# Reordering GpSimd's weight split, the stacking DMAs and the low parts of x in a decoder layer's attention

## The reference, cut to what matters

```
x = x + attention(layernorm(x), W_qkv, W_out)
  q, k, v = split(xn @ W_qkv)            # 16 heads of 64
  q, k = rotary(q), rotary(k)            # pairs of columns: x1*cos - x2*sin, x1*sin + x2*cos
  w = softmax(mask(q @ k.T / 8))         # causal
  out = (w @ v) @ W_out
x = x + memory_attention(layernorm(x), ctx)   # a scan over 64 context rows builds the memory
x = x + experts(layernorm(x))
```

## Time and profile before

| | |
|---|---|
| median of three runs | 2825.81 us |
| the profiled execution | 2824.66 us |
| its span | 2822.9 us |
| mean granted TensorE clock | 0.975 |
| TensorE busy | 2640.8 us (94%) |
| VectorE busy | 2004.1 us (71%) |
| ScalarE busy | 1620.0 us (57%) |
| GpSimd busy | 1497.6 us (53%) |

### The profile page before, as it was taken

One profiled execution on the slowest core, in us unless ns is written; L12 is line 12 of the kernel. 1 busy time (PEld: TensorE's weight loads), 2 busy tenths in 40 slices (PEclk: granted clock), 3 DMA queues, 4 the chain that ended last, 5 costly groups with the idle time before them and its releaser, 6 DMA issues. The chain is left out here.

```text
span 2822.9 us, 51923 instructions
## 1 busy us (share of the span) xinstructions
PE 2640.8 (94%) x16935; PEld 2336.0 (83%) x16935; DVE 2004.1 (71%) x4219; ACT 1620.0 (57%) x3158; POOL 1497.6 (53%) x1680
## 2 busy tenths in 40 slices
PE   8999989999899999899997799999969999999997
PEld 5888878888788888788886677778759999999997
DVE  6777777777767777777776688879856666666665
ACT  3666666666756666666665533333326666666665
POOL 3676746666556766577653334434424444444444
PEclk9999999999999999999998899999979999999999
DMA  6544443535443545343535454545334434444433
GB/s 170 115 116 116 108 121 91 123 99 128 115 100 88 132 103 125 101 113 84 117 75 139 119 180 144 146 131 149 116 132 104 102 74 89 102 103 104 104 53 52
DMA packets 192360, 316.56 MB, mean 112 GB/s; under 512 B 60496, under 2 KB 106224, under 8 KB 189104
## 3 DMA queue, kind: packets, MB, share of 16 engines
q1 hardware_dynamic: 148656, 216.86, 31.1%
q0 software_dynamic: 43520, 97.46, 14.0%
HBM read 241.08 MB, written 75.17 MB: 112 GB/s over the span
## 5 line engine op out<-in xcount | busy, mean ns | idle before, releaser
L1171 ACT ACTIVATE a_pt<-a_PT 128x512 fp32r<-128x512 f32 (+3 forms) x768 | 350.3, 490 | 466.1 <-PE a_PT L1030 461.0
L1316 DVE TENSOR_TENSOR a_pt<-a_PT,a_pt 128x512 fp32r<-128x512 f32 (+3 forms) x768 | 401.0, 549 | 154.2 <-ACT a_pt L1171 150.4
L1306 DVE CUSTOM_DVE_ANT_0 a_S<-a_S,a_mask 128x1024 f32<-128x1024 f32 (+7 forms) x512 | 386.9, 756 | 80.1 <-PE a_S L1019 78.7
L1160 ACT ACTIVATE a_pb<-a_S,a_nmax 128x1024 f32<-128x1024 f32 (+7 forms) x512 | 379.9, 742 | 26.4 <-DVE a_nmax L1306 24.5
L1030 PE MATMUL a_PT<-early_ident,a_pb 128*128 128x128 f32 x2304 | 342.9, 276 | 55.6 <-DVE a_pt L1316 55.2
L1030 PEld LDWEIGHTS a_PT<-early_ident,a_pb 128*128 128x128 f32 x2304 | 274.5, 142 | 111.5 <-issue 68.6
L1047 PE MATMUL a_O<-a_pt,a_v 128*128 128x256 f32 (+1 forms) x2560 | 344.6, 282 | 8.1 <-DVE a_xt L1291 5.3
L1047 PEld LDWEIGHTS a_O<-a_pt,a_v 128*128 128x128 f32 x2560 | 328.5, 192 | 20.8 <-DVE a_xt L1291 11.1
L1018 PE MATMUL a_S<-a_kh,a_qs 128*128 128x512 f32 (+3 forms) x768 | 283.0, 369 | 21.7 <-DMA a_kl<-early_rot 21.0
L2215 POOL DMA_INDIRECT early_stage<-in_we,e_ix x119 | 128.6, 1081 | 276.9 <-issue 140.1
L1019 PE MATMUL a_S<-a_kl,a_qs 128*128 128x512 f32 (+3 forms) x768 | 259.0, 349 | 0.0
(11 more groups left out here) (332 smaller groups left out, 7610.0 us busy)
## 6 DMA issues: line engine op xcount, KB each, us to landing
a_qs<-early_rot SPq DMA_DIRECT2D x256, 128.0 KB
a_kh<-early_rot SPq DMA_DIRECT2D x256, 128.0 KB
a_kl<-early_rot SPq DMA_DIRECT2D x256, 128.0 KB
m_hn<-scr_hs SPq DMA_DIRECT2D x40, 516.0 KB
scr_attT<-a_ot SPq DMA_DIRECT2D x256, 64.0 KB, 2.2
early_stage<-in_wqk POOLq DMA_DIRECT2D x31, 512.0 KB, 4.1
m_att<-scr_attT SPq DMA_DIRECT2D x30, 512.0 KB
m_rb<-scr_rinv SPq DMA_DIRECT2D x60, 256.0 KB
```

Source lines behind the costliest of these rows:

```text
L1160: act.activation(pb[u % 2][:, 0:cols], S[u % 2][:, 0:cols], ACT.Exp, bias=nmax[:, u % GU:u % GU + 1], scale=-1.0, accum_out=rsum[:, b % 2, ...
L1171: act.activation(pt[u % 2][:, 0, 4 * s:4 * s + m, (qt % 2) * P:(qt % 2 + 1) * P], PT[(k + s) % 2][:, 0:m * P].rearrange("p (k q) -> p k q" ...
L1306: dve.tensor_tensor_reduce(out=sc, in0=sc, in1=mask[:, T - cols:T], scale=-1.0, scalar=-MASKED, op0=ALU.add, op1=ALU.min, accum_out=nmax[: ...
L1316: dve.tensor_tensor(pt[u % 2][:, 1, 4 * s:4 * s + m, q], PT[(k + s) % 2][:, 0:m * P].rearrange("p (k q) -> p k q", k=m), pt[u % 2][:, 0, 4 ...
```

## The change

Five edits, all in the attention phase. On SP, a stack's first six DMAs wait for the rotation's high parts and the last six for the low parts. On GpSimd, the load behind the very first weight split waits for the first stack, and `load_next` for the stack of head 62; weights are split at the head of a step, ahead of the rotation's additions and low parts, while the loads behind x's parts keep their place. On ScalarE, before the loop, the values' first two high copies stand between and behind the two rotation copies and ahead of the weight copy. On VectorE, x's low parts move behind the values' and the probabilities' low parts of the step.

```diff
             def stack(hg):
                 i, sl = hg // 2, hg % 2
-                sp.wait_ge(s_rot, 4 * (i + 1))
                 if hg >= 2:
                     sp.wait_ge(s_sfull, QT * (hg - 1))
                 for r in range(4):
+                    if r == 0:
+                        sp.wait_ge(s_rhi, 4 * (i + 1))
+                    if r == 2:
+                        sp.wait_ge(s_rot, 4 * (i + 1))
                     sp.dma_start(qs[r * 32:r * 32 + 32, sl, :].bitcast(F32),
...
                 if p in ridx and ridx[p] + 2 < len(by_raw):
+                    if p == pieces[0]:
+                        gp.wait_ge(s_stack[0], 192)
                     load(ridx[p] + 2)
...
                 gp.wait_ge(s_wlow, len(wcount))
+                gp.wait_ge(s_stack[0], 192 * (last + 1))
                 for k in range(6):
...
             for u in range(U + 2):
+                for p in splits(u):
+                    if p[0] != "x":
+                        low(p)
                 for i, j in ends(q_steps(u - 1), 4):
                     if j % 2:
                         rope_add(i, j // 2)
...
                 for p in splits(u):
-                    low(p)
+                    if p[0] == "x":
+                        low(p)
...
             rope_high(0, 0)
+            v_high(0, 0)
             rope_high(0, 1)
+            v_high(0, 1)
             high(pieces[0])
-            for j in range(4):
+            for j in range(2, 4):
                 v_high(0, j)
...
                     tile_stats(tile_in(u, 4))
-                if 0 < u < U:
-                    for p in splits(u - 1):
-                        if p[0] == "x":
-                            x_low(p)
                 for i, j in ends(q_steps(u - 1), 4):
                     if j < 3:
                         rope_mult(i, j)
...
                 if 2 <= u < U + 2:
                     part_low(u - 2)
+                if 0 < u < U:
+                    for p in splits(u - 1):
+                        if p[0] == "x":
+                            x_low(p)
```

## The result

The changed kernel takes 2853.93 us (median of six runs, 2849.48 to 2855.60) against 2827.80 for the kernel before on the same chip (six runs, 2821.13 to 2831.80): ratio 1.0092, 95% interval 1.0077 to 1.0107. It is slower by 26 us; 2850 was forecast. The profiled execution of after has a span of 2852.3 us and a granted clock of 0.976, that of before 2822.9 and 0.975.

The account below looks back on a forecast made before the run. TensorE, busy 94% of the span, was taken to bound the kernel. Terms +46.1, +4, -10.7, -1.4, -10.0, -1.5 and -2 gave +24.5 us, 2850 on the median; 2822 to 2868 for eight times in ten.

Parts of the forecast that it names:

- The swap: Weight split ahead of GpSimd's additions: ScalarE's rotation copy comes late, delaying TensorE's product with the probabilities; +46.1 us.
- Rival 1: ScalarE's delay doesn't reach TensorE, the 0.12 us slack being a misreading; only the gains are left, 2800 us; chance 0.14.
- rival 2: Half the swap's delay arrives, TensorE making up the rest in its small waits; 2823 to 2838 us; chance 0.18.
- The 23 pairs: Ordinary pairs of heads in attention where the swap's delay reaches TensorE: 1.99 to 2.28 us each, together 48.4 us.
- The clock: TensorE's new idle gaps of 2 us can take its clock down; +4 us, at most 32.
- Rival 3: The clock falls in most of TensorE's new gaps; 2870 us or more; chance 0.06.
- Stacks: Stacking DMAs start on high parts, so eight head-change waits go: -10.7 us, and -1.4 for the clock's dip at 501.
- The end: Six loads wait for head 62's stack, so TensorE's wait near 1540 nearly goes; -10.0 us.
- The room of 2 us: At the end, the six loads run beside the last stack with about 2 us to spare; otherwise up to 9.8 return.
- rival 4: The three-megabyte load collides with the last stack: 9.8 us come back, 2859 us; chance 0.07.
- The opening: TensorE's 2.04 us wait at 57.48 goes with the values' copy earlier, projections end sooner; -1.5 us (0 to -2.5).
- The turns: Three batch turns: TensorE's waits shrink with x's low parts behind the probabilities', 0.7 us per turn; -2 us (0 to -9).

Follow-up runs that it names:

- load_behind: The changed kernel with the weight split still first, but the load that follows it issued behind the rotation's additions; 2823.91 us, ratio 0.9992 to the kernel before.
- no_swap: The changed kernel with GpSimd's old order put back (rotation's additions first, then weight split and load); 2801.93 us, ratio 0.9909 to the kernel before.
- swap_only: The kernel before with only the weight split moved ahead of the rotation's additions on GpSimd; 2868.08 us, ratio 1.0141.
- stack_only: The kernel before with only the stacks' split wait (first six DMAs on the high parts, last six on the low parts); 2808.84 us, ratio 0.9929.
- end_only: The kernel before with only the six 512 KB loads for the following phase waiting for head 62's stack; 2823.58 us, ratio 0.9977.
- x_only: The kernel before with only x's low parts moved behind the probabilities' low parts on VectorE; 2824.45 us, ratio 0.9988.
- swap_at_turns: The changed kernel with the weight split ahead of the additions only at the three batch turns, GpSimd's old order elsewhere; 2802.19 us, ratio 0.9902.

## Why the prediction was right

**The swap** was priced at 46.1 us plus 4 for the clock, 50.1; it measured 52. The step-by-step sum held in its parts: split to additions 3.26 us (3.35 forecast), wait of the copy 1.86 (2.05), gap of TensorE 1.80 to 2.0 (1.95), 0.10 us between VectorE's end and TensorE's start (0.12). The gap is that of 21 pairs. Rival 1, that this small slack was an artefact of modelled ends, falls with the gaps; rival 2, that half is made up in TensorE's small waits, falls with load_behind: even a delay of 0.94 us arrives whole. The 23 pairs were the right ones, and the six at and behind the turns swallowed their delay. One step was misread: all 23 pairs were priced with a load behind the split, and the last two (heads 58 and 60) have none, so 0.92 and 1.25 us arrived there in place of 1.9 and 2.2. The other 21 heads were priced at 42.0 us and grew by 43.3 without the dips. Their gaps are 39.5 of these; where TensorE lost the other 0.2 us a head isn't shown.

**The clock.** Of the 52.0 us the five heads with a dip hold 1.3 us each over their neighbours, 6.5 in all, against 4 forecast; the price of a dip (1.4) was right, and 45.5 remain for the gaps, against 46.1. Rival 3, a dip in most gaps, falls: behind 18 of the 23 gaps there was none.

**Stacks.** -12.1 forecast with the dip at 501. The eight heads between 6 and 42 gained 13.7 us in no_swap (18, the one with the dip, 3.45), so the term was right there. What the prediction didn't see is that the swap takes the same waits away: swap_only costs 40 us with the old stacks, which is 52 less these 12. So the two terms hold only as a pair. The swap's 50 is its price beside the stack edit, and beside the swap the stack edit is worth nothing at these heads. Alone in before the edit is worth 20 [14, 26]; a part of what it gained beyond the term, 3.0 us, lies at the end: 1.23 at head 62, where a stack that starts earlier meets the six loads earlier (8.5 us of waiting instead of 9.8), and 1.75 at head 63, the low clock's tail of before that stack_only hasn't. The SP queue ran as worked out: rotation copy 295.86, first stack DMA 3.2 us later (3.1 forecast), the last six 7.0 us later (7.0):

```profile
299.07 0.57 SPq L709 DMA_DIRECT2D a_qs<-early_rot  x1
...
302.86 0.59 SPq L709 DMA_DIRECT2D a_qs<-early_rot  x1
303.49 1.24 SPq L713 DMA_DIRECT2D a_kl<-early_rot  x2
```

**The end.** -10.0 forecast; -6.5 by the times of end_only, with 10 inside its interval, and 8.3, 9.9 and 8.6 us in heads 62 and 63 together of after, no_swap and end_only. The size was near, but two errors met. The room of 2 us for loads and last stack together wasn't enough, and a wait of 2.73 us stands in after, over a fourth of rival 4. Against it, the low clock behind the wait of before cost 1.75 us more than the 0.9 that was put in the sum. Before TensorE's first scores of the last head in after:

```profile
1566.97 3.18 POOL L897 DMA_DIRECT2D early_stage<-in_wmem  x6 [11.21 <-DMA a_kl<-early_rot]
...
1586.61 0.50 PE L1028 MATMUL a_S<-a_kh,a_qs 128*128 128x512 f32 x1 [2.73 <-DMA a_kl<-early_rot]
```

**The opening.** -1.5 forecast; heads 0 to 2 of after took 2.0 more (no_swap's 1.2), and alone it is nothing (+3 us at ratio 1.0011, zero within the interval). Taken from no_swap's heads, this is the term that was mis-sized most, by 2.7 us. Answers to the earlier trace rows:

```profile
55.18 1.23 DVE L1255 TENSOR_TENSOR scan_keys<-scan_keys,a_rT 128x1024 f32<-128x1024 f32 x1
...
64.02 0.50 PE L972 MATMUL a_Z<-early_xT,early_wq 128*128 128x512 f32 x1 [1.86 <-DVE a_v L1308]
...
95.57 0.33 PE L1040 MATMUL a_PT<-early_ident,a_pb 128*128 128x128 f32 x1 [3.70 <-DVE a_pt L1328]
```

The 2.04 us wait went and a like one of 1.86 appeared 6.5 us on, at the first projection with the next query-key weight, again for VectorE to free a bank of Z. The step that failed is that I stopped at the first stack: the next gate, x's tile behind SP's key loads, doesn't move with TensorE, and what is won before it is waited for there.
The key normalisation took 1.23 us instead of 3.01, having started before GpSimd. The rule of the Trainium skill ("SBUF — State Buffer", section "Who interferes with whom"), that the first of the two to start keeps the other out, agrees with that; the gain it would have added did not reach the end. A turn of before doesn't show the rule as plainly: there VectorE's 3.54 us subtraction and GpSimd's split start within 0.06 us, VectorE first by the records, and yet it is VectorE that ran long. GpSimd's times are rough, so the order can't be told from them.

**The turns.** -2 forecast; -5.7 in after's heads and -3.6 in x_only's (3.4 by the medians' ratio, zero at the edge of the interval). The step named as the cost is there: x's last low part moved back, and TensorE waited 1.55 us for it. The gain was underrated. The first two low parts took 2.28 and 1.38 us in after instead of 3.54 and 2.60, as they no longer ran beside GpSimd's split, which fits; but in x_only, where they took 2.47 and 2.01, the gain at this turn was 2.07 against 2.28, so how much of it is theirs isn't shown. Of the 5.7, 1.74 lie at the third turn, where x_only and no_swap gained nothing. Answers to the earlier trace rows:

```profile
390.05 2.28 DVE L1277 TENSOR_TENSOR early_xT<-early_stage,early_xT 128x1024 fp32r<-128x1024 f32 x1
395.40 1.38 DVE L1277 TENSOR_TENSOR early_xT<-early_stage,early_xT 128x1024 fp32r<-128x1024 f32 x1
...
401.92 0.38 PE L972 MATMUL a_Z<-early_wv,early_xT 128*128 128x256 f32 x1 [1.55 <-DVE early_xT L1277]
```

The gains came to 25.7 us (no_swap) against 25.6 forecast. That the sum is so close is luck in part: head by head in no_swap the opening was overrated by 2.7 us, the stacks and the turns each underrated by about 1.6, and the end was right. In the same way the two pairs without a load, 2 us too dear, were offset by dips that cost 2.5 more than forecast.

Left open: why SP's eight key loads take 7.2 to 10.3 us from kernel to kernel, what of stack_only's 20 us beyond 16.7 is real, and where the 3.4 us behind head 63 come from, which no_swap has as well (3.5).

## What to carry to other kernels

An edit on an engine that is half idle costs its full length where an in-order engine waits for it ahead of work that frees a buffer of the bound engine; follow the queue behind the waiter, and count how often. If the order is needed, move the waiter, not the work: putting one copy behind the freeing move turned 26 us of loss into 32 of gain. Two edits can cover the same wait: an edit that makes the bound engine late hides its waits for transfers, so price such edits together. An early gain is worth only what the next gate that doesn't move with it lets through.

## What the runs showed of the hardware

The same eight loads on SP's queue, issued at 75 to 81 us, took from 7.22 (before) to 10.31 us (swap_at_turns) to issue. Head 1 took from 22.9 to 27.5 us, on the whole longer where they did, which is more than the opening's edits are worth. And of 23 new gaps in TensorE, 21 of them of 1.80 to 2.00 us, five cost more than their length (1.3 us each), with a granted clock of 0.66 in the 5 us behind them, a mean over both its levels (1.2 and 2.4 GHz), where it is 1.00 behind the others: the same gap mostly leaves the clock alone and sometimes doesn't. Which head it hits changes from kernel to kernel: 6, 18, 28, 42 and 56 in after, 6, 26, 42, 50, 52 and 56 in swap_only, none of the ordinary heads in load_behind, whose gaps are about 1 us.
